# Keys times values by four column tiles of the PE array, in a kernel of two feed-forward layers around linear attention

## What is computed

```python
def attn(x, w_qkv, w_proj, b_proj):          # 16 heads of 32 channels
    qkv = (x @ w_qkv.T).reshape(B, N, 3, C)
    q, k, v = (qkv[:, :, 0], qkv[:, :, 1], qkv[:, :, 2])
    q, k, v = relu(to_heads(q)), relu(to_heads(k)), to_heads(v)
    v_pad = jnp.pad(v, ((0, 0), (0, 0), (0, 1), (0, 0)), constant_values=1.0)
    vk = jnp.einsum('bhen,bhdn->bhed', v_pad, k)
    out = jnp.einsum('bhed,bhdn->bhen', vk, q)
    out = out[:, :, :-1] / (out[:, :, -1:] + EPS)
    return out.reshape(B, C, N).transpose(0, 2, 1) @ w_proj.T + b_proj

x = x + 0.5 * ffn(layernorm(x), w_gate_up, w_proj)
x = x + attn(layernorm(x), w_qkv, attn_w_proj, b_proj)
x = x + 0.5 * ffn(layernorm(x), w_gate_up, w_proj)
```

## Time and profile before

| | us |
|---|---|
| three runs | 905.74, 903.67, 900.71 |
| median | 903.67 |
| the profiled execution | 901.2 |
| its span, from the first to the last instruction | 899.4 |
| TensorE busy in the span | 874.2 |
| VectorE, ScalarE, GpSimd busy | 477.8, 371.2, 71.5 |
| TensorE's granted clock, mean | 1.00 |

### The profile page before, as it was taken

How to read it: one execution, slowest core, us unless ns; L and a number is a source line. 1 busy time by engine, 2 the same in 40 slices (tenths; PEclk the granted TensorE clock), 3 DMA queues, 4 the chain that set the end, 5 groups by cost and what they waited for, 6 DMA issues and landing times.

```text
span 899.4 us, 11530 instructions
## 1 busy us (share of the span) xinstructions
PE 874.2 (97%) x4222; PEld 420.6 (47%) x4288; DVE 477.8 (53%) x978; ACT 371.2 (41%) x732; POOL 71.5 (8%) x106
## 2 busy tenths in 40 slices
PE   3989999999999999999999999999999999999998
PEld 2534444444444444455555555444444444444443
DVE  7999997834335455436373737454334344433232
ACT  6677567446344445202121212253333434343431
POOL 3211001201000000101000000000000001000000
PEclk9999999999999999999999999999999999999999
DMA  9987508996336688332222304034444433342235
GB/s 278 139 139 146 87 9 167 199 198 140 83 82 133 122 168 157 65 57 38 48 48 46 49 13 83 12 61 76 87 87 89 71 70 71 71 71 59 59 64 135
DMA packets 251384, 84.90 MB, mean 94 GB/s; under 512 B 237889, under 2 KB 240449, under 8 KB 251329
## 3 DMA queue, kind: packets, MB, share of 16 engines
q1 hardware_dynamic: 242704, 70.54, 41.2%
q0 software_dynamic: 3872, 4.72, 3.9%
q10 hardware_dynamic: 4752, 8.91, 3.2%
HBM read 25.43 MB, written 4.19 MB: 33 GB/s over the span
## 4 chain that ended last, share of the span: by engine, by line
PE 93%; DVE 4%; DMA 1%; issue 1%; ACT 0%; SPq 0%; DVEq 0%
PE proj_ps L1090 24%; PE up_ps L1076 22%; PE gate_ps L1076 22%; PE gate_ps L1182 7%; PE up_ps L1182 7%; PE proj_ps L1100 5%; PE proj_ps L1076 3%; PE proj_ps L1193 2%; PE gate_ps L1115 1%; PE up_ps L1115 1%; PE sum_ps L1062 1%; DMA xs<-xn 1%; DMA xs<-in_L_attn_x_dram 1%; DVE stats L769 0%; DVE att_w L851 0%
## 5 line engine op out<-in xcount | busy, mean ns | idle before, releaser
L1090 PE MATMUL proj_ps<-down_w,slots 128*128 128x512 bf16 x939 | 209.8, 379 | 1.1
L1076 PE MATMUL gate_ps<-gu_w,xT 128*128 128x512 bf16 (+1 forms) x885 | 201.7, 367 | 3.7 <-DMA xT<-xn 1.9
L1076 PE MATMUL up_ps<-gu_w,xT 128*128 128x512 bf16 (+1 forms) x891 | 202.1, 368 | 0.7
L790 DVE SCALAR_TENSOR_TENSOR slots<-up_ps,silu 128x512 f32<-128x512 f32 x118 | 81.6, 691 | 176.3 <-PE up_ps L1076 157.0
L1090 PEld LDWEIGHTS proj_ps<-down_w,slots 128*128 128x128 f16 x960 | 93.9, 98 | 112.8 <-DVE xs L812 0.2
L549 ACT ACTIVATE silu<-gate_ps 128x512 f32<-128x512 f32 x118 | 69.6, 590 | 167.0 <-PE gate_ps L1076 166.8
L1076 PEld LDWEIGHTS gate_ps<-gu_w,xT 128*128 128x128 f16 x904 | 86.1, 98 | 102.3 <-DMA xT<-xn 2.1
L1076 PEld LDWEIGHTS up_ps<-gu_w,xT 128*128 128x128 f16 x904 | 86.1, 98 | 99.1
L559 ACT ACTIVATE o_buf<-slots 128x512 f32<-128x512 f32 x128 | 80.4, 628 | 103.8 <-DVE slots L790 103.2
L812 DVE SCALAR_TENSOR_TENSOR xs<-proj_ps,xs 128x512 f32<-128x512 f32 x32 | 22.1, 691 | 136.1 <-PE proj_ps L1090 136.1
L803 DVE SCALAR_TENSOR_TENSOR slots<-slots,inv 128x512 f16<-128x512 f32 x124 | 91.0, 743 | 2.7 <-ACT slots L570 2.7
(11 more groups left out here) (103 smaller groups left out, 738.7 us busy)
## 6 DMA issues: line engine op xcount, KB each, us to landing
out_dram<-xs SPq DMA_DIRECT2D x16, 256.0 KB, 2.4
slots<-in_L_ffn_w_gate_up_dram ACTq DMA_DIRECT2D x6, 512.0 KB, 7.8
aw_raw<-in_L_attn_w_qkv_dram ACTq DMA_DIRECT2D x12, 256.0 KB, 2.8
aw_raw<-in_L_attn_w_qkv_dram SPq DMA_DIRECT2D x12, 256.0 KB, 3.0
xs<-in_L_attn_x_dram SPq DMA_DIRECT2D x2, 1024.0 KB, 6.6
slots<-slots SPq DMA_TRANSPOSE x76, 4.5
xs<-in_L_attn_x_dram ACTq DMA_DIRECT2D x1, 1024.0 KB, 12.3
aw_raw<-in_L_ffn_w_gate_up_dram POOLq DMA_DIRECT2D x4, 256.0 KB, 7.3
```

Source lines behind the costliest of these rows:

```text
L790: nc.vector.scalar_tensor_tensor(out=h_rows(i, q), in0=bank(up_ps, j), scalar=GU_OUT, in1=silu_rows(j), op0=ALU.mult, op1=ALU.mult).then_i ...
L1076: mm = nc.tensor.matmul(bank(ps, j)[:, first:first + width], xT(m)[:, t, r, k, :], gu_w[:, k, c:c + width], start=(k + r == 0), stop=(k == ...
L1090: mm = nc.tensor.matmul(proj_ps[:, use % 2, :], h_turned(i)[:, r, j, :], down_w[:, j, :], start=(r + j == 0), stop=(r == 1 and j == HC - 1))
```

## The change

Keys times values is done head by head. For each token tile and each head one matmul has 32 columns of K as the stationary operand and the 32 V channels of that head with a column of ones, 33 columns, as the moving one. The four heads of a chunk write the PSUM partitions 0, 32, 64 and 96, that is, each uses its own 32 columns of the array with all 128 rows. V is stored with a column of ones behind each head (`V_W` = 33). `kv_rhs` becomes a buffer of its own, cleared once by GpSimd; VectorE copies the blocks onto its diagonal, four copies of 32 partitions. The masks and the multiplications with them go. Keys times values moves from behind u = 5 to ahead of it, on TensorE and on VectorE. The Q product keeps its shape, with its 132 columns in another order.

```diff
-KV_W = P + HPG
-V_W = P + 1
-V_TILE = DC * V_W
+HEADS = DC * HPG
+V_W = HEAD + 1
+KV_W = HPG * V_W
+V_TILE = HEADS * V_W
...
-        mask = sb("mask", [P, P], F32)
-        mask4 = sb("mask4", [P, HPG], F32)
+        kv_rhs = sb("kv_rhs", [P, DC, KV_W], F32)
...
-        kv_rhs = silu[:, :, :].rearrange("p a n -> p (a n)")[:, 0:DC * KV_W]\
-            .rearrange("p (g m) -> p g m", g=DC)
...
             for p in range(PE_TURNED + 7, PIECES):
                 load_piece(p)
+            nc.gpsimd.memset(kv_rhs[:, :, :], 0.0).then_inc(kv_zeroed, 1)
...
-            nc.vector.memset(mask4[:, :], 0.0)
-            nc.vector.memset(group_ones[:, :], 0.0)
-            step.done(nc.vector.memset(mask[:, :], 0.0))
-            for h in range(HPG):
-                nc.vector.memset(mask[h * HEAD:(h + 1) * HEAD, h * HEAD:(h + 1) * HEAD], 1.0)
-                nc.vector.memset(mask4[h * HEAD:(h + 1) * HEAD, h:h + 1], 1.0)
+            step.done(nc.vector.memset(group_ones[:, :], 0.0))
...
+                    if u == 5:
+                        if b == 0:
+                            dve.wait_ge(kv_zeroed, 1)
+                        dve.wait_ge(proj_done, KV_USE[b] + 2)
+                        for e in range(HPG):
+                            rows = slice(e * HEAD, e * HEAD + HEAD)
+                            last = nc.vector.tensor_copy(
+                                kv_rhs[rows, :, e * V_W:e * V_W + V_W].rearrange("p (c g) m -> p c g m", c=2),
+                                proj_ps[rows, :, 0:2 * V_W].rearrange("p c (g m) -> p c g m", g=2))
+                        last.then_inc(proj_used, 2)
                     dve.wait_ge(up_done, att_pair(b) + u + 1)
...
-                use = KV_USE[b]
-                for half in range(2):
-                    dve.wait_ge(proj_done, use + half + 1)
-                    kv = proj_ps[:, (use + half) % 2, 0:2 * V_W].rearrange("p (g m) -> p g m", g=2)
-                    nc.vector.tensor_tensor(kv_rhs[:, 2 * half:2 * half + 2, 0:P], kv[:, :, 0:P],
-                                            mask[:, :].rearrange("p (o m) -> p o m", o=1).broadcast_to([P, 2, P]),
-                                            ALU.mult)
-                    for g in range(2):
-                        last = nc.vector.tensor_scalar(kv_rhs[:, 2 * half + g, P:KV_W], mask4[:, :], kv[:, g, P:V_W],
-                                                       None, ALU.mult)
-                    last.then_inc(proj_used, 1)
...
                         for t in range(TILES):
-                            mm = nc.tensor.matmul(proj_ps[:, (use + half) % 2, c:c + V_W],
-                                                  k_tile(t)[:, g * P:(g + 1) * P], v_tile(t)[:, g, :],
-                                                  start=(t == 0), stop=(t == TILES - 1))
+                            for e in range(HPG):
+                                at = g * P + e * HEAD
+                                mm = nc.tensor.matmul(proj_ps[e * HEAD:e * HEAD + HEAD, half, c:c + V_W],
+                                                      k_tile(t)[:, at:at + HEAD], v_tile(t)[:, HPG * g + e, :],
+                                                      start=(t == 0), stop=(t == TILES - 1))
                     mm.then_inc(proj_done, 1)
+
+            for b in range(BLOCKS):
+                for u in range(5):
+                    qkv(b, u)
+                keys_values(b)
+                qkv(b, 5)
```

More of the change, by code:

```diff
@@ L973, in attention_output @@
                 dve.wait_ge(up_done, j + 1)
-                halves = (out_half(t).rearrange("p (g m) -> p g m", g=2),
-                          up_ps[:, j % 2, 0:2 * KV_W].rearrange("p (g m) -> p g m", g=2))
+                halves = (out_half(t).rearrange("p (h m) -> p h m", h=2 * HPG),
+                          up_ps[:, j % 2, 0:2 * KV_W].rearrange("p (h m) -> p h m", h=2 * HPG))
                 dve.wait_ge(gate_used, j + 1 + CREDIT)
                 for s in range(2):
-                    last = nc.vector.tensor_scalar(
-                        den[:, 8 * s:8 * s + 8].rearrange("p (g h) -> p g h", g=2),
-                        halves[s][:, :, P:KV_W], den_eps[:, 0:1], None, ALU.add)
+                    last = nc.vector.tensor_scalar(den[:, 8 * s:8 * s + 8], halves[s][:, :, HEAD], den_eps[:, 0:1],
+                                                   None, ALU.add)
                 step.done(last)
@@ L1009, in _ @@
                             for c in (2 * (u - 2), 2 * (u - 2) + 1):
[L1010 to L1012 removed]
+                                nc.vector.memset(v_tile(c)[:, :, HEAD:V_W], 1.0).then_inc(ones_placed, 1)
+                        nc.vector.tensor_scalar(v_tile(2 * (u - 2) + 1)[:, :, 0:HEAD],
+                                                up_ps[:, u % 2, :].rearrange("p (h m) -> p h m", h=HEADS), QKV_OUT,
                                                 None, ALU.mult).then_inc(up_used, 1)
@@ L1166, in _ @@
                 pe.wait_ge(awT_here[k], 16 * UNITS // 2)
-            for b in range(BLOCKS):
-                for u in range(6):
-                    for ps, done, used, side in ((gate_ps, gate_done, gate_used, 0), (up_ps, up_done, up_used, 1)):
-                        part, c = u // 2, 2 * (u % 2) + side
-                        pe.wait_ge(used, att_pair(b) + u + 1)
-                        if part == 0:
-                            pe.wait_ge(xT_here[c], 16 * (5 + b))
-                        terms = [(k, r, s) for k in range(DC) for r, s in ((0, 0), (0, 1), (1, 0))]
-                        for m, (k, r, s) in enumerate(terms):
-                            if part < 2:
-                                lhs, dst = xT0[:, c, r, k, :], ps[:, u % 2, :]
-                                rhs = att5[:, s, k, 4 * (part + 1):4 * (part + 2), :].rearrange("p u m -> p (u m)")
-                            else:
-                                lhs, rhs = att5[:, s, k, c, :], xT0[:, :, r, k, :]
-                                dst = ps[:, u % 2, :].rearrange("p (t q) -> p t q", t=TILES)
-                            mm = nc.tensor.matmul(dst, lhs, rhs, start=(m == 0), stop=(m == len(terms) - 1))
-                        mm.then_inc(done, 1)
-                use = KV_USE[b]
@@ new lines, in qkv @@
+            def qkv(b, u):
+                for ps, done, used, side in ((gate_ps, gate_done, gate_used, 0), (up_ps, up_done, up_used, 1)):
+                    part, c = u // 2, 2 * (u % 2) + side
+                    pe.wait_ge(used, att_pair(b) + u + 1)
+                    if part == 0:
+                        pe.wait_ge(xT_here[c], 16 * (5 + b))
+                    terms = [(k, r, s) for k in range(DC) for r, s in ((0, 0), (0, 1), (1, 0))]
+                    for m, (k, r, s) in enumerate(terms):
+                        if part < 2:
+                            lhs, dst = xT0[:, c, r, k, :], ps[:, u % 2, :]
+                            rhs = att5[:, s, k, 4 * (part + 1):4 * (part + 2), :].rearrange("p u m -> p (u m)")
+                        else:
+                            lhs, rhs = att5[:, s, k, c, :], xT0[:, :, r, k, :]
+                            dst = ps[:, u % 2, :].rearrange("p (t q) -> p t q", t=TILES)
+                        mm = nc.tensor.matmul(dst, lhs, rhs, start=(m == 0), stop=(m == len(terms) - 1))
+                    mm.then_inc(done, 1)
@@ L1188, in _ @@
                 for half in range(2):
-                    pe.wait_ge(proj_used, use + half + 1)
+                    pe.wait_ge(proj_used, KV_USE[b] + half + 1)
                     for g in (2 * half, 2 * half + 1):
```

16 lines of the change are left out of this document (9 added, 7 removed).

## The result

| | before | after |
|---|---|---|
| median, us | 902.76 (6 runs) | 893.62 (6 runs) |
| lowest and highest | 900.71 to 905.74 | 891.93 to 897.3 |
| ratio, with 95% interval | | 0.9907 (0.989 to 0.9925) |
| profiled execution, span | 901.2, 899.4 | 892.16, 890.4 |

The forecast was 906.1 us, with a range of 897 to 921. The kernel is faster than the range's lower end, and in the direction that had been given 13 in 100.

A forecast was written before the change was run, and what follows sets the result against it. The prediction took TensorE to bound the kernel. Tiles at +1.1 us and switches of shape at +1.3 us gave +2.4 us on 903.67 us, so 906.1 us, with a range of 897 to 921 us.

The forecast's parts named there:

- The stage is TensorE's alone: Attention stage: a microsecond of TensorE time is a microsecond of the kernel; TensorE busy 49.00 of 49.00 us a block.
- Two passes for an f32 product: Keys times values: each f32 product runs as two passes, each with its own weight load; 512 matmuls and loads expected.
- 30 ns of streaming for 33 columns: Narrow keys-times-values pass: 33 columns at 0.83 ns each plus 2.5 ns fixed, 30 ns.
- the tiles: Keys times values as 128 narrow passes a block, tiles taking turns at 30 ns a pass: +1.1 us in four blocks.
- lower bound: Narrow pass on four tiles: at least 15 ns, 1.92 us a block, as each product's two passes share a tile.
- The switches: TensorE going between whole array and column tiles, 8 times at 0.16 us each: +1.3 us (0 to 3.0).
- The place: Keys times values moved ahead of u = 5, its copies of about 1 us lying under u = 5's 5.18 us: nothing.
- The copy of Q: VectorE's copy of Q behind u = 5, 0.69 us, keeps some 1.9 us of slack: nothing.
- the x transposes: SyncE's transposes of x behind u = 5, needed 3.6 us sooner, still finish in time: nothing.
- The fast one: Keys times values: tiles stream at once, 15 ns a pass, 1.92 us a block; kernel 898.4 us, chance 0.22.
- The slow one: Keys times values: a floor or visible load makes a pass 57 to 60 ns; about 920 to 921 us, chance 0.32.
- The granted clock: Attention stage: clock falls to 1.2 GHz, +15 us; chance 0.04 together with a lost cover or anything else.

The follow-up runs named there:

- e1: Changed kernel with keys times values on the whole array again (32 passes of 132 columns), still moved and without mask: ratio to before 0.9993.
- e5: Changed kernel with all 128 passes of a block on the first column tile, each head's token tiles in a row: ratio to before 1.0043.
- e6: Changed kernel streaming 66 columns a pass (own head and neighbour) on four tiles: 14.4 ns a pass, 2.07 us net a block, one run, no ratio.
- e2: Changed kernel with two loops swapped, so eight passes in a row go to one column tile: 20.3 ns a pass, ratio to before 0.9965.
- e3: Changed kernel with keys times values and its copies put back behind u = 5: ratio to before 0.9959.
- e9: Changed kernel with K and V stored as fp16, 64 passes of 33 columns a block on four tiles: ratio to before 0.9861.
- e10: Changed kernel with keys times values on the whole array, 132 columns, and K and V in fp16, 16 passes a block: ratio to before 0.9889.
- e4: Changed kernel with two column tiles of 64, two heads each, 64 passes of 66 columns a block: 29.6 ns a pass, ratio to before 0.9942.
- e7: Changed kernel with 17 streamed columns instead of 33, half the output not computed: 8.8 ns a pass, 1.32 us net a block, one run, no ratio.

## Why the prediction was wrong, step by step

- **The stage is TensorE's alone: right.** 8.9 of 9.0 us are the net time of keys times values, and e1 shows that nothing else in the change moves the end.
- **Two passes for an f32 product: right.** The line has 512 matmuls and 512 loads.
- **30 ns of streaming for 33 columns: right** within 2 ns for one tile (31.9 in e5), and with 66 columns and four tiles, 57.5 / 4 ns, to the tenth (e6).
- **The step that failed is the price of a pass with four tiles**, the term "the tiles", put at +1.1 us. Its lower bound was 15 ns, by this argument: the two passes of a product use one tile at 30 ns each, so "the next tile starts its first pass no sooner than the second pass of the one before". Measured are 8.8 ns. The argument took starts in program order to mean that a waiting pass holds up everything behind it. e2 shows that it doesn't until three passes wait on a tile: the next tile starts while they do. With that bound gone, four tiles give 30 / 4 = 7.5 ns, and a floor for handing out, which turned out at 8.8, would have been the limit to look for. A row that pointed at it was there: two queued f32 loads of 128 columns start 0.06 us apart, a quarter is 15 ns; but the bf16 loads beside them start 0.01 to 0.02 us apart with a matmul between, and these I set aside.
- **The value chosen inside the bounds was wrong as well.** 30 ns meant that tiles take turns. The argument for it, that every row "follows the column count", came from rows in which only the whole array is used, and they can't tell turns from overlap. The term was +1.1 us and measured 4 x (1.14 - 3.57), about -9.7 us (1.14 us are 128 passes at 8.9 ns). This makes 10.8 of the 12.5 us by which the forecast missed. The switches make 0.4, and 0.9 is the starting point: 903.67 from three runs of the kernel before, 902.76 from six.
- **The switches: right in kind**, +1.3 us forecast. The net time less the passes, 1.35 - 1.14 = 0.21 us a block, is +0.9 us.
- **The place at nothing: right, for the reason given,** the cover of u = 5. The copies took 1.21 us (forecast: 1 us). e3 prices that cover at 5.6 us of waiting, which the prediction had not worked out. The copy of Q ends at 439.23 in block 1 and is needed at 440.93, 1.7 us later (forecast 1.9); the x transposes end at 443.99 and are needed at 452.46.
- **The rivals.** The fast one was the right mechanism with the wrong floor: 898.4 us, where without the bound of 15 ns its own sum, at 7.5 ns a pass, gives 4 x (0.96 - 3.57) + 1.3 = -9.1 us and 894.5. Its condition, tiles that stream at once, had no row for or against; 0.22 was too little for that. The slow one falls: the load doesn't show in each pass, even on a single tile (31.9 ns against 30). It seems to show once, at the start of a run: 53 ns from a tile's first start to its second. The Trainium skill's rule behind it, that loads overlap with matmuls in flight only when the row group differs ("TensorE: Matmul & The Clock Gate", Part 3), does not hold here, since all passes use all rows. The rule of the same part that put the fast rival forward, matmuls on different tiles starting about 4 ns apart, agrees with the first passes of a run: the first four start 3 to 4 ns apart in e9, where a product is one pass, and 6 to 7 ns apart in f32, where it is two. It isn't the pace of the whole run, 8.8 ns. The granted clock stayed at 1.00, the 2.4 GHz level, throughout the attention.

## What to carry to other kernels

If blocks of a product are thrown away afterwards (a diagonal, a mask), giving each block its own column tile can pay on a TensorE-bound kernel; count the passes, take for each the larger of its streaming time over the number of tiles and the pace of handing out, here 8.8 ns, and spread neighbouring passes over different tiles, since the same passes in another loop order cost twice as much (e2, 2.79 against 1.35 us net). Look then at what the long product used to hide: the copy of its result needs other work to lie under. And weigh a cheaper operand type first where precision allows it: one pass of fp16 on the whole array (e10) takes 0.92 us net a block, where f32 on four tiles takes 1.35. The kernel times alone don't tell the two apart (0.9889 and 0.9907, with overlapping intervals).

## What the runs showed of the hardware that I had not expected

- A start shown for a matmul on a column tile is when the tile takes it up. On one tile none are closer than 29 ns (e5); on four, the first four start within 0.02 us.
- Passes overtake each other across tiles: a tile starts while three passes handed out earlier still wait for another (e2).
- The second pass on a tile comes late, and later with a wider load: 53 ns after the first with 32 columns of load and 33 streamed (e5), 81 with 32 and 66 (e6), 108 with 64 and 66 (e4). So 32 more columns of load cost 27 ns, once in a run of passes; afterwards the load is hidden.
- With four tiles a load and a matmul together take 8.8 ns in f32, the mean of 128 passes, and 7.9 ns in fp16, the mean of 64. Fewer columns don't help: 17 columns as 33 (e7).
- Two tiles of 64 and four tiles of 32 that stream 66 columns each take nearly the same time: 64 passes of 29.6 ns against 128 of 14.4, 2.11 and 2.07 us net.
- Going from the whole array to tiles and back costs about 0.12 us each time.
